# One state's inflow product of the selective scan made by GpSimd from du and a broadcast row of B, TensorE making nine in place of ten

## What is computed

```python
def step(h, inp):
    u_t, d_t, b_t, c_t = inp
    dA = jnp.exp(d_t[..., None] * A)                 # decay
    dBu = (d_t * u_t)[..., None] * b_t[:, None, :]   # inflow
    h = dA * h + dBu
    y = jnp.einsum('bdn,bn->bd', h, c_t)
    return (h, y)
# ... then  y = (y + u * D_skip) * silu(z);  out = y @ out_proj_w.T;  x = x + out
```

## Time and profile before

| | |
|---|---|
| median of 3 runs | 5272.86 us (5270.67 to 5282.67) |
| the profiled execution | 5273.96 us, of which the span from first to last instruction is 5272.2 |
| mean granted TensorE clock | 0.965 of full speed |
| busy, share of the span | PE 88%, DVE 75%, POOL 69%, ACT 66%, PEld 65% |
| first slot of chunks 1, 8, 9 and 15 | at 443, 2353, 2623 and 4257 us |
| end of the last scan | 4481 us |

### The profile page before, as it was taken

How to read it: one execution, slowest core, us unless ns; L and a number is a source line. 1 busy time by engine, 2 the same in 40 slices (tenths; PEclk the granted TensorE clock), 3 DMA queues, 4 the chain that set the end, 5 groups by cost and what they waited for, 6 DMA issues and landing times. The chain is left out here.

```text
span 5272.2 us, 90572 instructions
## 1 busy us (share of the span) xinstructions
PE 4649.4 (88%) x26392; PEld 3440.3 (65%) x26392; DVE 3947.5 (75%) x4317; ACT 3497.5 (66%) x6211; POOL 3635.1 (69%) x2906
## 2 busy tenths in 40 slices
PE   1798989898989898989898989999898988798998
PEld 0566666666666666666666666666666667586786
DVE  4788979898988888888888898989798988212212
ACT  1676767676767676777777777767676766463663
POOL 1477778777777777777777777777777789332432
PEclk8899999999999999999999999999999999999999
DMA  5102020201010201010101001010102010323313
GB/s 191 53 1 65 5 66 5 62 9 62 9 62 9 62 9 58 13 58 13 58 13 47 24 29 41 20 49 13 58 4 67 4 59 7 116 64 104 104 56 112
DMA packets 119824, 245.61 MB, mean 47 GB/s; under 512 B 10496, under 2 KB 11648, under 8 KB 117728
## 3 DMA queue, kind: packets, MB, share of 16 engines
q1 hardware_dynamic: 110816, 222.30, 12.9%
q10 hardware_dynamic: 8448, 16.78, 0.9%
HBM read 204.44 MB, written 34.60 MB: 45 GB/s over the span
## 5 line engine op out<-in xcount | busy, mean ns | idle before, releaser
L704 POOL TENSOR_TENSOR hc<-hs,c_rows 128x512 f32<-128x512 f32 x2048 | 2598.1, 1278 | 931.9 <-DVE hs L659 456.7
L659 DVE TENSOR_TENSOR_SCAN hs<-da,carry,bank 128x512 f32<-128x512 f32 x1280 | 1630.9, 1274 | 213.7 <-PE bank L742 110.4
L742 PE MATMUL bank<-b_diag,du_t 128*128 128x128 f32 x10240 | 1425.2, 284 | 282.3 <-ACT du_t L540 183.9
L742 PEld LDWEIGHTS bank<-b_diag,du_t 128*128 128x128 f32 x10240 | 1287.6, 197 | 347.4 <-issue 178.2
L846 PEld LDWEIGHTS bank<-identity,hc 128*128 128x128 f32 x8192 | 1016.9, 144 | 664.4 <-issue 558.3
L846 PE MATMUL bank<-identity,hc 128*128 128x128 f32 x8192 | 1251.3, 277 | 17.0 <-ACT sp_l L548 12.3
L444 ACT ACTIVATE da<-delta,neg_a 128x512 f32<-128x512 f32 x1280 | 906.1, 716 | 192.0 <-DVE hs L659 190.4
L659 DVE TENSOR_TENSOR_SCAN hs<-bank,carry,hs 128x512 f32<-128x512 f32 x768 | 962.3, 1266 | 0.5
L444 ACT ACTIVATE bank<-delta,neg_a 128x512 f32<-128x512 f32 x768 | 526.3, 685 | 555.0 <-DVE hs L659 443.0
L1017 POOL TENSOR_TENSOR xg_low<-xg,xg_high 128x512 fp32r<-128x512 f32 x192 | 248.5, 1295 | 473.3 <-ACT xg_high L1041 465.7
L647 DVE TENSOR_TENSOR hs<-bank,b_rows 128x512 f32<-128x512 f32 x768 | 518.3, 675 | 73.2 <-POOL hc L704 56.1
(11 more groups left out here) (160 smaller groups left out, 5882.5 us busy)
## 6 DMA issues: line engine op xcount, KB each, us to landing
c_rows<-b_and_c_rows SPq DMA_DIRECT2D x256, 256.0 KB, 3.5
xl<-x SPq DMA_DIRECT2D x48, 1024.0 KB, 5.6
b_rows<-b_and_c_rows SPq DMA_DIRECT2D x96, 256.0 KB, 3.6
c_rows<-in_x SPq DMA_DIRECT2D x8, 2048.0 KB, 8.2
xn<-in_x ACTq DMA_DIRECT2D x16, 1024.0 KB, 7.4
xres<-in_x SPq DMA_DIRECT2D x64, 256.0 KB, 3.1
x<-xres SPq DMA_DIRECT2D x64, 256.0 KB, 2.0
out<-keys SPq DMA_DIRECT2D x16, 1024.0 KB, 5.0
```

Of the source, the lines that this page charges most:

```text
L659: dve.tensor_tensor_scan(hs[:, n % H_RING, :], decay, inflow, carry[:, STATE * j + n:STATE * j + n + 1], ALU.mult, ALU.add).then_inc(h_rea ...
L704: pool.tensor_tensor(hc[:, n % HC_RING, :], hs[:, n % H_RING, :], c_rows[:, n, :], ALU.mult).then_inc(hc_ready, 1)
L742: mm = pe.matmul(x_ps[ring_bank(nn)][:, q * P:(q + 1) * P], du_t[:, jn % 2, q * P:(q + 1) * P], b_diag[:, w, q, :], start=True, stop=True)
```

## The change

State 3 leaves BY_TENSOR and becomes BY_POOL. Its row of B joins `b_rows`, which grows from six rows to seven; `b_diag` shrinks from ten to nine. POOL makes the inflow in its slot 1, ahead of its L704 of that slot, from `du` and the row, into `hs`. DVE's scan of state 3 waits for that (`pool_dbu`) and reads its decay from a PSUM bank, so ACT writes exp(3) there.

```diff
-BY_TENSOR = (0, 1, 3, 4, 6, 7, 9, 10, 12, 13)
+BY_TENSOR = (0, 1, 4, 6, 7, 9, 10, 12, 13)
+BY_POOL = (3,)
+ROWS = BY_VECTOR + BY_POOL
...
     # SyncE: loads of the rows
-                            if n in BY_VECTOR:
-                                v = BY_VECTOR.index(n)
-                                wait(sp, dbu_ready, N_V * (JT * (c + 1) - 1) + v + 1)
+                            if n in ROWS:
+                                v = ROWS.index(n)
+                                if n in BY_VECTOR:
+                                    wait(sp, dbu_ready, N_V * (JT * (c + 1) - 1) + v + 1)
+                                else:
+                                    wait(sp, pool_dbu, N_P * (JT * (c + 1) - 1) + BY_POOL.index(n) + 1)
...
     # ScalarE: the decay
-                                act.activation(x_ps[ring_bank(nn)][:, :] if nn in BY_VECTOR else da[:, nn % X_RING, :],
+                                act.activation(da[:, nn % X_RING, :] if nn in BY_TENSOR else x_ps[ring_bank(nn)][:, :],
...
     # VectorE: the scan
+                                elif n in BY_POOL:
+                                    dve.wait_ge(pool_dbu, N_P * tile + BY_POOL.index(n) + 1)
+                                    decay, inflow = x_ps[ring_bank(n)][:, :], hs[:, n % H_RING, :]
...
     # GpSimd: the product
+                            if scan and n + 2 in BY_POOL:
+                                nn = n + 2
+                                if j == 0:
+                                    pool.wait_ge(b_loaded[ROWS.index(nn)], 16 * (c + 1))
+                                wait(pool, hc_ready, step + 3 - H_RING)
+                                wait(pool, carried, STEPS // 2 * c + (slot + 2 - H_RING) // 2 + 1)
+                                pool.tensor_tensor(hs[:, nn % H_RING, :], du[:, :], b_rows[:, ROWS.index(nn), :],
+                                                   ALU.mult).then_inc(pool_dbu, 1)
```

More of the change, by code:

```diff
@@ L28 @@
 BY_VECTOR = (2, 5, 8, 11, 14, 15)
-BY_TENSOR = (0, 1, 3, 4, 6, 7, 9, 10, 12, 13)
-N_V, N_T = len(BY_VECTOR), len(BY_TENSOR)
+BY_TENSOR = (0, 1, 4, 6, 7, 9, 10, 12, 13)
+BY_POOL = (3,)
+ROWS = BY_VECTOR + BY_POOL
+N_V, N_T, N_P = len(BY_VECTOR), len(BY_TENSOR), len(BY_POOL)
 Y_AFTER, DU_AFTER = 5, 13
@@ L172, in mamba_and_linear_attention @@
             c_rows = sb("c_rows", [P, STATE, T], layer0)
-            b_rows = sb("b_rows", [P, N_V, T], layer0)
+            b_rows = sb("b_rows", [P, len(ROWS), T], layer0)
             b_diag = sb("b_diag", [P, N_T, BLOCKS, P], layer0)
@@ L329, in mamba_and_linear_attention @@
             c_loaded = [sem(f"c_loaded{n}") for n in range(STATE)]
-            b_loaded = [sem(f"b_loaded{v}") for v in range(N_V)]
+            b_loaded = [sem(f"b_loaded{v}") for v in range(len(ROWS))]
+            pool_dbu = sem("pool_dbu")
             dt_mm = sem("dt_mm")
@@ L440, in scalar_chunk @@
                                     act.wait_ge(delta_ready, tile + 2)
-                                wait(act, h_ready, step + (3 - scans_before(nn) if nn in BY_VECTOR else 0) if scan else 0)
-                                if nn == Y_AFTER + 3 and nn in BY_VECTOR:
+                                wait(act, h_ready, step + (0 if nn in BY_TENSOR else 3 - scans_before(nn)) if scan else 0)
+                                if nn == Y_AFTER + 3 and nn not in BY_TENSOR:
                                     wait(act, y_skip, tile)
-                                act.activation(x_ps[ring_bank(nn)][:, :] if nn in BY_VECTOR else da[:, nn % X_RING, :],
+                                act.activation(da[:, nn % X_RING, :] if nn in BY_TENSOR else x_ps[ring_bank(nn)][:, :],
                                                delta[:, jn % 2, :], ACT.Exp,
```

## The result

The changed kernel takes 5246.28 us (median of 5 runs, 5238.69 to 5258.78); the kernel before, timed beside it, 5274.26 (5270.67 to 5282.67). The ratio is 0.9944, interval 0.9933 to 0.9955: 28 us by the medians, 0.6% faster by the ratio.

The account below looks back on a forecast made before the run. No engine bounds the whole chunk; PE, DVE and POOL take turns. Chunks 1 to 14 give 32.9 us, chunk 0 0.2, chunk 15 -0.1: 33.0 off 5273.96 is 5241, 5240 as median (1.1 lower); range 5195 to 5285.

Parts of the forecast that it names:

- the 0.96 that would have spoken for the clock: Whole run: a mean granted clock under 0.96 would be a sign that the clock took the gain.
- PE late in tile 2: Tile 2, slot 1: PE starts state 4's product late, so all 0.89 us of removed PE work are gained.
- the waits at state 4: Tiles 1, 3, 5 and 7: PE's waits on DVE at state 4 grow, gain nil.
- Tile 6: Tile 6, ahead of state 4's product: PE is late as in tile 2, so 0.89 us are gained again.
- second rival: PE's saving becomes waits in tiles 2 and 6 (5264), or the clock falls, 1.6 us a chunk (5265); chance 0.20.
- The diagonal: Tile 7, on DVE: one diagonal fewer a chunk, 0.57 us on the path.
- POOL's product: Slot 1 of each tile: POOL's extra 1.24 us fits its 2.8 us of gaps; no DVE wait in most tiles.
- 0.6 us of margin: Tile 2: POOL's inflow is ready 0.6 us before DVE's scan of state 3 starts.
- The wait for the turned y: DVE's wait for L718 falls by about 0.9 us in tiles 2 and 6, some 25 us in all.
- Chunk 15: POOL loses 3 x 1.24 = 3.7 us in tiles 4 to 6, PE gains 3.6 in tiles 0 to 3: -0.1.
- Chunk 0: One tile of each kind and one diagonal: 0.89 - 1.24 + 0.57 = 0.2 us gained.
- The first: Tiles 2 and 6: POOL becomes the bound, its product delaying L647, 1.9 us a chunk, 5309 us; chance 0.18.
- The third: All tiles: all of PE's saving counts, 123 us, giving 5150; more gain, below 5225, had chance 0.14.

Follow-up runs that it names:

- pe_twice_4: The changed kernel, but PE makes the product of state 4 twice in its slot 2: 5300.07 us, ratio 1.0035.
- pool_added: The kernel before, plus POOL's product and DVE's wait for it; PE still makes ten products and the scan reads PE's: 5278.75 us, ratio 1.0003.
- diag_once: The kernel before, but the diagonal of state 3 is made for the first chunk only: 5268.34 us, ratio 0.9983.
- dt_fill: The changed kernel, but in tile 5, slot 14, PE makes the dt product five times, ahead of the waiting inflow product: 5225.41 us, ratio 0.9893.
- pool_state4: The changed kernel, but POOL makes the product of state 4 in place of state 3's: 5202.59 us, ratio 0.9853.
- pool4_dt_first: State 4 on POOL in place of state 3, and slot 14's dt product, made once, ahead of the inflow product in every scan tile: 5193.72 us.

## Why the prediction was right, step by step

The forecast was 5240 with 5195 to 5285; the median is 5246. Most steps held. The mean granted clock came to 0.967, not under the 0.96 that would have spoken for the clock. That the sum came out so near is luck in part: in the profiled run the steady tiles gave 29 us of the 33, and tile 0 (12.7) and the start (4.9), which the forecast had at nothing, stood against chunks 0 and 15 and the end (11.7).

**PE late in tile 2: right.** 33.03 to 32.13, forecast 0.89, measured 0.90, in every chunk. For tiles 1 and 3 nil was forecast and 0.11 and 0.01 measured, and the waits at state 4 took up all 0.89 as said. Tiles 4 and 5: nil and nil. In tiles 5 and 7 PE idled about 0.9 us more in the slot of that wait (0.5 to 1.4 and 0.3 to 1.1, from the timelines), also as said.

**Tile 6: the term held, the clock moved around it.** It gained 0.57 us, forecast 0.89. That the two are near is in part luck: two effects of the clock, neither of them in the sum, pull against each other. In three parts (means of chunks 1 to 14, from the timelines): slots 0 to 5 take 11.96 before and 11.93 after, slots 6 to 14 take 17.47 in both, and from slot 15 to the next tile 2.39 and 1.84. At half clock, which is what the changed kernel always has here, the first part went from up to 12.83 to 11.94, the 0.89 of the forecast. But before, half of the chunks had full clock and 11.17. The gain was given back by more falls. At the other end of the tile the clock gave some of it back. The last items of tile 6 in chunk 8, before and after:

```profile
2588.19 2.07 PE L742 MATMUL bank<-b_diag,du_t 128*128 128x128 f32 x8 [2.66 <-ACT du_t L540]
```

```profile
2590.30 0.69 DVE L630 TENSOR_TENSOR b_diag<-identity,bank 128x512 f32<-128x512 f32 x1 [0.53 <-PE bank L742]
```

```profile
2561.77 1.34 PE L759 MATMUL bank<-b_diag,du_t 128*128 128x128 f32 x8 [2.66 <-ACT du_t L546]
```

The same eight products took 2.07 us before and 1.34 after, behind the same idle time. Before, DVE's first diagonal of the next tile waits 0.53 for them, and from slot 15's scan to the next tile are 2.39 us in all 14 chunks; after, it doesn't wait in chunk 8, and the step is 1.75 in 12 of 14. In my second rival I had priced a clock that falls more often at 1.6 us a chunk. It fell more often in one place (the first part kept only 0.03 of its 0.89, so 0.86 a chunk were given back) and later in another (0.55 gained): -0.89 + 0.86 - 0.55 = -0.58. Why the clock falls more often after a change that leaves this stretch as it was stays open; pe_twice_4 and pool_added, each with a part of the change, have 8 and 10 falls and not 14. The rule as I used it in that rival, that added waiting costs clock, did not hold in tile 3: it waits 0.89 us more and kept 1.00.

**The diagonal: right in its slot.** The step that held it is 0.58 us shorter, forecast 0.57. The whole tile 7 is 0.48 shorter, and 0.40 in diag_once, with a doubt of over 0.2 on each, as tile 7 scatters with the clock. DVE's next diagonal now waits longer for PE: L636 in tile 7, 0.21 us before and 1.02 after in chunk 8.

**POOL's product: ready in time in tile 2, but not in tile 0.** I had said that most tiles would have no wait for the new product, and that is so. But tile 0 has one in 11 of the 13 chunks; I hadn't looked at it in this respect. Timeline of tile 0 in chunk 8, after:

```profile
2329.37 1.27 POOL L721 TENSOR_TENSOR hc<-hs,c_rows 128x512 f32<-128x512 f32 x1 [3.27 <-issue]
...
2330.60 1.28 POOL L714 TENSOR_TENSOR hs<-du,b_rows 128x512 f32<-128x512 f32 x1
...
2331.98 1.28 DVE L668 TENSOR_TENSOR_SCAN hs<-bank,carry,hs 128x512 f32<-128x512 f32 x1 [2.46 <-POOL hs L714]
```

POOL begins its chunk 4 us after DVE: its first `hc` product stands behind 3.27 us in which it waits for nothing that the profile shows, at the turn of the loop over chunks. In tiles 1 and 3 to 7 of chunks 2 to 14 the product is there. In tile 2 the forecast's 0.6 us of margin was gone in chunk 8, behind a half clock in tile 1 (0.91 for the tile), and in chunk 14: the scan waited 0.4 us. The length of tile 2 doesn't show it (32.12 to 32.15 in all 14 chunks).

```profile
2404.27 1.28 POOL L714 TENSOR_TENSOR hs<-du,b_rows 128x512 f32<-128x512 f32 x1
...
2405.65 1.28 DVE L668 TENSOR_TENSOR_SCAN hs<-bank,carry,hs 128x512 f32<-128x512 f32 x1 [0.42 <-POOL hs L714]
...
2411.29 0.75 DVE L615 SCALAR_TENSOR_TENSOR xs<-xs,skip,bank 128x512 f32 x1 [1.33 <-PE bank L735]
...
2425.19 0.69 DVE L653 TENSOR_TENSOR hs<-bank,b_rows 128x512 f32<-128x512 f32 x1 [1.27 <-POOL hc L721]
```

L615 waits 1.33 us there against 1.84, and L653 1.27 for POOL in both kernels (in 13 chunks there are 29 waits in place of 26, the three new ones in tile 0): in tile 2, the gaps between slots swallowed the product, as the forecast had it. Whether the waits of tile 0 cost anything can't be said, since its mean is uncertain by 0.3 us.

**The wait for the turned y: right in tile 2, wrong in tile 6.** I said that it would fall by some 25 us in all; it fell by 7 in 13 chunks. In tile 2 it fell by 10.8 us, 0.83 a tile, nearly the forecast's 0.9. In tile 6 it rose by 3.6, where the first part of the tile ran at half clock in every chunk. The larger fall of the wait for inflow products is mostly tile 0's, where DVE waits for POOL in place of PE, and is no measure of the gain.

**Chunk 15: POOL's term too large, and the clock left out.** Forecast 0.1 us lost, measured 4.0. PE's part (3.6 gained in tiles 0 to 3) holds at full clock: in dt_fill tiles 0 to 3 are each 0.9 shorter than before. Tile 1 of chunk 15, after, and the same tile in dt_fill, where the clock stayed up (before: 30.31 us at 1.00):

```profile
4242.49:4273.55 31.06, 30.30 (x178) 22.57 (x177) 25.62 (x28) 20.35 (x37) 27.46 (x23) 0.95 0.05 18
```

```profile
4238.26:4267.66 29.40, 28.66 (x176) 20.93 (x175) 25.52 (x27) 20.23 (x37) 27.45 (x23) 1.00 0.06 20
```

After, the clock fell in tiles 0 and 1 and took 1.7 us of each, and again in tile 5 (0.85). POOL's part was sized too large. I charged 1.24 us in each of tiles 4 to 6, 3.7 in all. dt_fill has the same product on POOL and kept full clock for all of chunk 15; against before, its tile 4 is 0.96 longer, tile 5 0.28 longer and tile 6 0.15 shorter, 1.1 in all. pool_added gives the same for tiles 4 and 5 (0.95 and 0.24). The kernel before did not have full clock in these tiles (0.94, 0.89 and 0.92), so 1.1 may be somewhat too low. Tile 6, after and in dt_fill:

```profile
4387.67:4416.09 28.42, 22.27 (x159) 18.29 (x158) 24.27 (x25) 19.82 (x35) 26.97 (x22) 0.98 0.00 1
```

```profile
4379.76:4407.02 27.26, 20.77 (x155) 17.20 (x154) 24.06 (x26) 20.20 (x37) 27.18 (x23) 1.00 0.00 1
```

So the 1.0 by which tile 6 grew after is not POOL's product; it goes with the lower clock in tiles 5 and 6. What the changed kernel lost to dt_fill in this chunk, 6.5 us, is the term that the forecast had at nothing: -3.6 + 1.1 + 6.5 = 4.0. pool_added lost 4.2 us in chunk 15, but 3.1 of them in tiles 6 and 7, with the clock at 0.85 and 0.98. Chunk 0, forecast 0.2 shorter, was 1.7 longer; why isn't shown.

**The rivals.** The first did not come true with one product, and in tile 2 it did with two. The second was true in tile 6 in so far as the clock took the gain back; why it fell isn't shown. The third falls with tiles 1 and 3, but its idea is worth having: pool_state4 shows 73 us by the medians for the same work in another slot.

## What to carry to other kernels

Where an engine stands at a wait, work taken from ahead of the wait is worth nothing, and work taken from behind it can be worth all: 0.01 against 0.93 us in tile 3, for the same 0.89 us of PE. Behind the wait is not enough by itself: state 6, later still, gave tile 3 its 0.90 too, but tile 2 nothing. So before moving one of several like operations to an idle engine, look in each stage for those that follow the wait of the late engine, and among them for one behind which the other engine still has gaps (that this is what state 6 lacks in tile 2 fits its longer waits for POOL, but no run took it apart). The slower engine can take the work as long as its gaps hold it (one product a tile cost nothing, the second nearly doubled the wait for POOL). Changes of under 1% have to be read per stage and beside the granted clock, as it can add or take 1.6 us a place.

## What was not expected of the hardware

- The same stretch of PE work, with the same idle time of 2.7 us in it (before, chunk by chunk), was followed by either level of the clock. It fell in 7 of 14 before, 14 of 14 after, 8 in pe_twice_4, 10 in pool_added, 9 in diag_once, 9 in dt_fill, 5 in pool_state4 and 1 in pool4_dt_first, in one execution of each. The price is 1.6 to 1.7 us for each.
- Elementwise work on POOL costs nearly twice as much as on DVE (1276 ns against 675 for a product of 128x512 f32), and still the kernel got faster. The Trainium skill (GPSIMD Engine Reference, section "Engine selection") gives VectorE for elementwise work and puts GpSimd at some 2x its time with two inputs; the trace agrees on the ratio, 1.9, and the run of pool_added shows that the product costs nothing where GpSimd isn't the late engine. No run gave the product to VectorE, so that GpSimd was the better of the two isn't shown.
- At the turn of the loop over chunks (chunk 8, after) POOL starts late, with 3.27 us in which it waits for nothing that the profile shows; DVE idles 2.48 us in the same way but begins 4 us earlier, and so it waits for POOL there.
